# One order of a vision layer's attention steps: both images' scores together, both images' weighted sums together

## The chip, the cores and the metric

One core of a Trainium2 chip runs the program. The metric is the device time in microseconds, as the median of several executions. In the text an *image* is one of 16 inputs of 256 tokens, and a *pair* is two images that are worked on together (pairs 0 to 7).

## The reference

The layer cuts images of 5x128x128 into 256 patches and embeds them to 256 features with a layer norm. Then follows attention with a decay in place of a softmax, for 16 heads of 64, and then a mixture of 8 experts of which each token uses two. Cut to the attention, which the change is about:

```python
q, k = silu(x @ Wq), silu(x @ Wk);  v = x @ Wv          # 16 heads of 64
cum = cumsum(-softplus(x @ Wa + ba), axis=1)
decay = exp(where(causal, cum[i] - cum[j], -inf))
attn = (q @ k.T) * decay
o = attn @ v
o = group_norm(o) * gn_w + gn_b
out = (o * sigmoid(x @ Wg)) @ Wo
```

After it come a residual, a layer norm, a router (softmax, the two best of eight), and for each expert gelu(x w1 + b1) w2 + b2, weighted and added to the residual.

## The kernel before

The order of work is written out by hand, engine by engine, with semaphores between the engines. All eight pairs go through eight steps each (`step(p, c)`, c from 0 to 7; the last one is `last_step(p)`). A step works on two heads, c for both images of pair p. Work of other stages rides along in the steps: the embedding of the next pair (`tokens`, `embed`, `embed_norm`, `turn`, `scaled_h`), the norm, gate and output projection of the pair before (`gn_mean`, `gated`, `y_hi`, `y_lo`, `out_proj`, `residual`, `turn2`), and the routing of that pair and the one before it (`route`, `keep_logits`, `choose`, `place`, `scatter`).

In a step TensorE computes the scores of image u (`scores`, L1246 to L1258) into banks 4 and 5, one for each head; the projections for the two heads of step c+1 (`queries` into bank 0, `keys` into bank 1, `gates` into bank 2, L1212 and L1219; `values` into bank 0, 1 or 2), each of six matmuls, since an operand is split into a high and a low part; and the weighted sums (`weighted`, L1260 to L1274) into bank 3. Scores use 64 rows of the array for each head and weighted sums 64 columns for each head, so that the two heads' matmuls run beside each other; everything else uses the full 128x128. An f32 matmul of the trace's "x4" rows is two passes.

The order of TensorE in a plain step is: scores of image 0, queries, weighted sum of image 0, scores of image 1, keys, gates, weighted sum of image 1.

ScalarE computes tanh of q, k and g (`tanh_q` L828, `tanh_k` L833, `tanh_g` L840), exp of the decay rows (`decay`, L858, four to an image and step), and copies of v (L849) and o (`keep_o`, L863). `tanh_q` and `tanh_k` share one buffer, so that `tanh_k` waits for `silu_q`. VectorE computes `silu_q` and `silu_k` (L1731, L1738) and the product of scores and decays (`decayed`, L1747), two to an image. The product goes into a buffer for each head, `att`, which is why it waits for the weighted sum before it. GpSimd masks the decay rows (`decay_rows`, L684), two to an image, does the powers of the norms (L690, L695, L699) and scatters the normed rows to the experts' lists (`scatter`, L706). Each engine works through its list in order: an instruction that waits holds all behind it. The decay rows come from memory into a ring of `RING` = 4 slots, issued by SyncE two steps ahead, when the products have left a slot (`load_decay`).

After the attention come the experts' blocks: full blocks of 256 rows (`whole_row`, `mixed_row`: `layer1`, `layer2`, split operands) and unit blocks of 128 rows (`one_row`: `one1`, `one2`, plain f32), in turn at the end. Their sums leave PSUM with the bias added on VectorE (`keep_y`, L2004), are weighted on GpSimd (L735) and added to the output by an indirect DMA (L741, `add_rows`), each after the one before has landed. The last round is one full block and one unit block.

## Time and profile before

| | us |
|---|---|
| median of 3 runs | 1272.64 (1271.24 to 1274.25) |
| the profiled execution | 1270.91 |
| its span, first to last instruction | 1268.7 |
| TensorE busy | 1244.9 (98%) |
| ScalarE busy | 857.0 (68%) |
| VectorE busy | 827.5 (65%) |
| GpSimd busy | 429.8 (34%) |

The span has three parts: a start of 36.5 us, the attention steps to about 792, and the experts' blocks to the end. Matmuls are pipelined in the trace: a row of the timeline runs on under the next, so that the difference of two starts is what a group takes. The granted clock of TensorE is given as a share of its full 2.4 GHz.

### The profile page before, as it was taken

What the parts mean: (1) busy time and instruction counts of PE and PEld (TensorE: products, weight loads), DVE (VectorE), ACT (ScalarE), POOL (GpSimd) and SP (SyncE); (2) the same over time, 40 slices, a digit from 0 to 9 for tenths busy, and PEclk for the clock granted to TensorE, in tenths of its full rate; (3) what the DMA queues carried; (4) which work ended last, traced back from release to release, by engine and by line L of the source; (5) the groups of instructions that cost most, each with busy time, mean ns of one, the idle gap of its engine ahead of it and who ended that gap; (6) DMA issues with size and microseconds to landing.
All of it is one profiled execution on the core that took longest, in us unless ns stands there. A gap on an engine that the chain in (4) does not pass through costs nothing. (4 is left out here: it accounts for less than half of the span.)

```text
span 1268.7 us, 27357 instructions
## 1 busy us (share of the span) xinstructions
PE 1244.9 (98%) x8554; PEld 1070.0 (84%) x8554; DVE 827.5 (65%) x2123; ACT 857.0 (68%) x2019; POOL 429.8 (34%) x524
## 2 busy tenths in 40 slices
PE   8999999999999999999999999999999999999996
PEld 6677788787877877878877877989999999999995
DVE  5555565666667666666666566657888888566562
ACT  4766666667658567567577566547888888666672
POOL 2211121242142141242241241354454454443434
PEclk9999999999999999999999999999999999999998
DMA  5532222233233242232231337388988886999983
GB/s 191 169 106 81 95 90 89 83 114 111 81 116 111 67 130 87 85 124 78 93 126 49 124 109 231 111 230 241 300 223 246 226 223 188 260 273 277 262 244 86
DMA packets 125607, 194.46 MB, mean 153 GB/s; under 512 B 16272, under 2 KB 91504, under 8 KB 125360
## 3 DMA queue, kind: packets, MB, share of 16 engines
q1 hardware_dynamic: 110864, 175.37, 43.5%
q0 software_dynamic: 13584, 17.26, 6.8%
q8 instruction: 54, 0.88, 0.3%
q10 hardware_dynamic: 1056, 0.55, 0.2%
q14 instruction: 49, 0.40, 0.1%
HBM read 167.40 MB, written 29.05 MB: 155 GB/s over the span
## 5 line engine op out<-in xcount | busy, mean ns | idle before, releaser
L1219 PE MATMUL bank<-xn_sp,big_r 128*128 128x512 f32 x1152 | 312.5, 408 | 1.0 <-DVE xn_sp L1719 1.0
L1219 PEld LDWEIGHTS bank<-xn_sp,big_r 128*128 128x128 f32 x1152 | 204.9, 189 | 54.2 <-issue 1.7
L1747 DVE TENSOR_TENSOR att<-bank,dec_x 128x384 f32<-128x384 f32 x256 | 130.4, 550 | 99.2 <-PE bank L1258 94.3
L858 ACT ACTIVATE dec_x<-dec_x,ncum 128x256 f32<-128x256 f32 (+1 forms) x512 | 189.8, 445 | 5.8 <-POOL dec_x L684 5.8
L684 POOL TENSOR_SCALAR_AFFINE_SELECT dec_x<-dec_x 128x256 f32<-128x256 f32 x256 | 110.0, 458 | 215.1 <-DMA dec_x<-cum_scratch 214.7
L1565 PE MATMUL bank<-big_r 128*128 128x256 f32 x1296 | 167.5, 285 | 1.6 <-DVE big_r L2016 1.6
L1565 PEld LDWEIGHTS bank<-big_r 128*128 128x128 f32 x1296 | 160.4, 192 | 2.9 <-DVE big_r L2016 2.0
L741 POOL DMA_INDIRECT out<-mid_f,tok x71 | 120.4, 1696 | 59.8 <-issue 20.3
L735 POOL TENSOR_SCALAR mid_f<-mid_f,dec_x 128x256 f32<-128x256 f32 x71 | 75.8, 1073 | 169.8 <-DVE mid_f L2004 167.4
L928 ACT ACTIVATE mid_f<-bank,h 128x256 f32<-128x256 f32 x216 | 101.3, 479 | 33.6 <-PE bank L1565 20.0
L828 ACT ACTIVATE tq<-bank 128x512 f32<-128x512 f32 x64 | 38.3, 598 | 113.0 <-PE bank L1219 112.9
L2020 DVE TENSOR_TENSOR big_r<-mid_f,big_r 128x256 fp32r<-128x256 f32 x216 | 91.1, 424 | 33.8 <-ACT big_r L948 33.7
L2011 DVE TENSOR_TENSOR big_r<-big_f,big_r 128x512 fp32r<-128x512 f32 x148 | 102.0, 693 | 9.7 <-ACT big_r L922 2.2
L1297 PEld LDWEIGHTS bank<-big_r,y_sp 128*128 128x128 f32 x768 | 95.5, 191 | 1.9
L1212 PE MATMUL bank<-big_r,xn_sp 128*128 128x512 f32 x384 | 97.0, 392 | 0.0
L1297 PE MATMUL bank<-big_r,y_sp 128*128 128x256 f32 x768 | 96.8, 284 | 0.0
L833 ACT ACTIVATE tq<-bank 128x512 f32<-128x512 f32 x64 | 38.2, 597 | 86.1 <-PE bank L1219 86.0
L922 ACT ACTIVATE big_r<-big_f 128x512 fp32r<-128x512 f32 x148 | 93.7, 637 | 2.8 <-DMA big_f<-in_L_ffn_w 2.6
L948 ACT ACTIVATE big_r<-mid_f 128x256 fp32r<-128x256 f32 x216 | 91.9, 426 | 0.0
L1255 PE MATMUL bank<-q_s,k_s 64*128 64x256 f32 x512 | 90.0, 428 | 0.3 <-DVE k_s L1738 0.3
L706 POOL DMA_INDIRECT expert_rows<-xn,slot x64 | 65.5, 1023 | 72.9 <-DVE slot L1882 56.7
L1269 PE MATMUL bank<-att,mid_f 128*64 128x256 f32 x512 | 84.8, 404 | 3.9 <-DVE att L1747 2.8
(237 smaller groups left out, 2225.4 us busy)
## 6 DMA issues: line engine op xcount, KB each, us to landing
big_f<-in_L_ffn_w SPq DMA_DIRECT2D x68, 1024.0 KB, 7.3
dec_x<-cum_scratch SPq DMA_DIRECT2D x128, 384.0 KB, 3.6
big_w<-in_L_ffn_w SPq DMA_DIRECT2D x12, 1024.0 KB, 7.7
mid_f<-expert_rows SPq DMA_DIRECT2D x27, 261.0 KB, 3.1
h_scratch<-h SPq DMA_DIRECT2D x16, 256.0 KB, 2.2
h<-h_scratch SPq DMA_DIRECT2D x8, 512.0 KB, 4.4
out<-h SPq DMA_DIRECT2D x16, 256.0 KB, 4.0
xt<-in_x SPq DMA_DIRECT2D x14, 256.0 KB, 3.8
```

The source lines that it names most:

```text
L684: pool.affine_select(out=d, in_=d, pattern=[[0, 2], [1, P]], compare_op=ALU.is_ge, fill=fill, base=0, channel_multiplier=-1).then_inc(M["c ...
L741: pool.indirect_dma_start(out=out_rows, out_offset=bass.IndirectOffsetOnAxis(ap=tok[k.par][:, s:s + 1], axis=0), in_=yo[k.par][:, s, :], i ...
L858: act.activation(d, d, ACT.Exp, bias=ncum[p % 2][:, NS * u + s, 2 * c + hh:2 * c + hh + 1]).then_inc(M["exp_done"], 1)
L922: act.activation(parts[0].rearrange("p k n -> p (k n)")[:, cols], staged[:, cols], ACT.Copy).then_inc(M[f"{name}_hi"], 1)
L928: act.activation(target, bank[hbank[c % HB]][:, 0:width], ACT.Gelu_apprx_tanh, bias=b1_sb[k.par][:, c:c + 1]).then_inc(M["gel_done"], 1)
L948: act.activation(g_sp[0][:, c, :], gel[c % NGEL], ACT.Copy).then_inc(M["gh_done"], 1)
L1212: mm = pe.matmul(bank[target][:, :], xp[:, k, t * P:(t + 1) * P], wp[:, k, n * 512:(n + 1) * 512], start=(k == 0 and j == 0), stop=(k == E ...
L1219: mm = pe.matmul(bank[target][:, :], wp[:, k, c * P:(c + 1) * P], xp[:, k, :], start=(k == 0 and j == 0), stop=(k == EC - 1 and j == 2))
L1297: mm = pe.matmul(bank[target][:, s * E:(s + 1) * E], yp[:, j, u * S + s * P:u * S + (s + 1) * P], wp[:, GC * g + j, :], start=(j == 0 and ...
L1565: mm = pe.matmul(bank[hbank[c % HB]][:, 0:BLK], wp[:, i, c * P:(c + 1) * P], xp[:, i, :], start=(i == 0 and j == 0), stop=(i == EC - 1 and ...
L1747: dve.tensor_tensor(att[hh][:, :], bank[4 + hh][:, 0:LW], dec[n % RING][:, hh, :], ALU.mult).then_inc(M["mult_done"], 1)
L2011: dve.tensor_tensor(lo, staged[:, cols], f32(hi), ALU.subtract).then_inc(M[f"{name}_lo"], 1)
```

## The change

- TensorE's plain step becomes: scores of image 0, scores of image 1, gates, queries, keys, weighted sum of image 0, weighted sum of image 1. The scores of image 1 go to the banks of queries and keys (0 and 1; in the very first step 6 and 3).
- `queries` and `keys` of the next step therefore wait for the third and the fourth product of this one; `values` always go to bank 2.
- VectorE's product overwrites the decay row in its slot, the buffers `att` are gone, and the ring has five slots, which come free after the weighted sum.
- ScalarE's order: the decay of the next step's image 0 and tanh of g stand ahead of tanh of q (in step 5 and in the very first step it stays behind); `keep_x2` of the second image and `xn_hi` move; `decay` of image 1 stays behind tanh of k.
- VectorE does the four products first in a step, with `affine_steps`, `spread`, `running_sums` and the rest behind; `keep_logits` of the first image comes behind `silu_q` in step 6.
- The last step of a pair, and the first expert block's early part (`turn_first` into bank 6), follow the same pattern.
- In the last round both halves of the full block's second layer come before the unit's first layer, and VectorE multiplies with the weights while it reads PSUM (`weighted_bias`, `keep_weighted`), so that GpSimd only scatters.

The removed lines of `step` and `last_step` are left out: they are the lines of the kernel before that do not return.

```diff
@@ -46,7 +46,7 @@
-RING = 4
+RING = 5
...
@@ -328,6 +327,12 @@
             if n > 0:
                 eng.wait_ge(M[name], n)
+        def score_bank(p, c, u, hh):
+            if u == 0:
+                return bank[4 + hh]
+            return bank[(6, 3)[hh]] if p == 0 and c == 0 else bank[hh]
         def pair(n):
             return 0 <= n < NPR
...
@@ -387,7 +392,7 @@
             def load_decay(p, c, u):
                 n = 2 * NP * p + 2 * c + u
-                have(sp, "mult_done", 2 * (n - RING + 1))
+                have(sp, "o_ps", n - RING + 1)
                 sp.wait_ge(M[f"cum_out{u}"], 48 * (p + 1))
                 rows = cum_d[p, u:u + 1, 2 * c:2 * c + 2, :].rearrange("a h n -> a (h n)")
                 sp.dma_start(dec[n % RING].rearrange("p h n -> p (h n)"), rows.broadcast_to([P, 2 * LW])).then_inc(M[f"dec_in{n % RING}"], 16)
...
@@ -948,62 +963,67 @@
                 act.activation(g_sp[0][:, c, :], gel[c % NGEL], ACT.Copy).then_inc(M["gh_done"], 1)
             def last_step(p):
+                nxt = pair(p + 1)
+                keep_o(p, 6)
+                if pair(p - 1):
+                    keep_x2(2 * p - 1)
+                y_hi(p, 0, 0)
                 if nxt:
+                    tanh_g(p + 1, 0)
                     y_hi(p, 0, 1)
                     tanh_q(p + 1, 0)
                     keep_v(p + 1, 0, 2)
+                    tanh_k(p + 1, 0)
+                    keep_v(p + 1, 1, 2)
                     decay(p + 1, 0, 0)
+                    decay(p + 1, 0, 1)
+                else:
+                    x_early(0)
                     keep_o(p, 7)
+                    y_hi(p, 0, 1)
                     active_early(0, 0)
             def step(p, c):
+                nxt, post, routed = pair(p + 1), pair(p - 1), pair(p - 2)
                 if c == 7:
                     last_step(p)
                     return
+                if c > 0:
                     keep_o(p, c - 1)
+                elif post:
+                    keep_o(p - 1, 7)
                 if c == 4 and nxt:
                     keep_xnT(2 * p + 3)
                 if c == 6 and post:
                     keep_x2(2 * p - 2)
                 if c == 5 and nxt:
                     softplus(p + 1)
+                late = c == 5 or (p, c) == (0, 0)
+                if not late:
                     decay(p, c + 1, 0)
+                tanh_g(p, c + 1)
                 if c in (1, 2) and post:
                     affined(p - 1, 1, c - 1)
                 if c == 3 and post:
                     y_hi(p - 1, 1, 1)
+                if c == 6:
                     affined(p, 0, 0)
+                tanh_q(p, c + 1)
+                if c == 0 and p > 0:
+                    keep_v(p, 2, 2)
+                if c in (1, 2, 3):
+                    keep_v(p, {1: 4, 2: 6, 3: 7}[c], 2)
+                tanh_k(p, c + 1)
+                if c == 0 and p > 0:
+                    keep_v(p, 3, 2)
+                if c == 1:
+                    keep_v(p, 5, 2)
+                if c == 6 and nxt:
+                    keep_cum(p + 1)
+                    xn_hi(p + 1)
+                if late:
+                    decay(p, c + 1, 0)
+                decay(p, c + 1, 1)
                 if c == 0 and routed:
                     top_exp(2 * p - 4)
                     top_exp(2 * p - 3)
...
@@ -1011,12 +1031,8 @@
                     y_hi(p - 1, 1, 0)
                 if c == 3 and nxt:
                     scaled_h(2 * p + 3)
-                if c == 6 and nxt:
-                    keep_cum(p + 1)
-                if c == 6 and main:
+                if c == 6:
                     affined(p, 0, 1)
-                if main:
-                    tanh_g(p, c + 1)
                 if c == 1 and nxt:
                     keep_xnT(2 * p + 2)
                     scaled_h(2 * p + 2)
...
@@ -1225,52 +1241,60 @@
                     pe.wait_ge(M["ws_lo"], 1)
                 pe.wait_ge(M["xl_done"], p + 1)
                 have(pe, "sq_done", NP * p + c)
-                have(pe, "v_done", 2 * TP * p + {1: 2, 3: 6, 4: 7}.get(c, 0))
+                if (p, c) != (0, 1):
+                    have(pe, "mult_done", 4 * (NP * p + c - 1) + 3)
                 project(0, 0, c, "q_ps")
             def keys(p, c):
                 if p == 0 and c == 0:
                     pe.wait_ge(M["ws_lo"], 3)
                 have(pe, "sk_done", NP * p + c)
-                have(pe, "v_done", 2 * TP * p + {1: 4}.get(c, 0))
+                if (p, c) != (0, 1):
+                    have(pe, "mult_done", 4 * (NP * p + c - 1) + 4)
                 project(1, 1, c, "k_ps")
             def gates(p, c):
                 if p == 0 and c == 0:
                     pe.wait_ge(M["ws_lo"], 4)
+                pe.wait_ge(M["xl_done"], p + 1)
                 have(pe, "tg_done", NP * p + c)
-                have(pe, "v_done", 2 * TP * p + {0: 1, 1: 3, 2: 5, 4: 8}.get(c, 0))
+                have(pe, "v_done", 2 * TP * p + {0: 0 if p > 0 else 1, 1: 2, 2: 4, 3: 6, 4: 7, 5: 8}.get(c, 0))
+                have(pe, "h2a_done", 2 * p if c == 1 else 0)
                 project(2, 3, c, "g_ps")
...
+                    pe.matmul(score_bank(p, c, u, hh)[:, 0:S], k[r, 0:P], q[r, :], start=True, stop=True)
+                    pe.matmul(score_bank(p, c, u, hh)[:, S:LW], k[r, P:S], q[r, P:S], start=True, stop=True).then_inc(M["s_ps"], 1)
...
@@ -1384,97 +1414,83 @@
             def last_step(p):
                 main, nxt = pair(p), pair(p + 1)
+                scores(p, 7, 0)
+                scores(p, 7, 1)
                 if pair(p + 2):
                     tokens(2 * p + 4)
+                if pair(p - 1):
                     route(2 * p - 1)
+                if p == NPR - 1:
+                    turn_first()
                 if nxt:
+                    gates(p + 1, 0)
                     queries(p + 1, 0)
+                    values(p + 1, 0, 2, "tg_done", NP * (p + 1) + 1)
                     keys(p + 1, 0)
+                    values(p + 1, 1, 2, "v_done", 2 * TP * (p + 1) + 1)
                     out_proj(p, 0, 0, 7, "lg_done", 2 * p)
+                    out_proj(p, 0, 1, 2, "v_done", 2 * TP * (p + 1) + 2)
+                weighted(p, 7, 0)
+                weighted(p, 7, 1)
+                if p == NPR - 1:
+                    early1(0, 0)
             def step(p, c):
+                nxt, post, routed = pair(p + 1), pair(p - 1), pair(p - 2)
                 if c == 7:
                     last_step(p)
                     return
+                scores(p, c, 0)
+                scores(p, c, 1)
+                gates(p, c + 1)
                 if c == 1 and routed:
                     ranks(p - 2, *(("gv_done", 2 * p) if post else ("taken_done", p - 2)))
                 if c == 2 and nxt:
                     tokens(2 * p + 3)
                 if c == 4 and post:
                     out_proj(p - 1, 1, 0, 7, *(("taken_done", p - 1) if routed else ("gv_done", 2 * p)))
+                if c == 5:
                     gn_mean(p, 0, "h2_done", 2 * p)
                 if c == 6 and nxt:
                     cum(p + 1)
                 if c == 6 and post:
                     route(2 * p - 2)
+                queries(p, c + 1)
+                if c == 0 and post:
+                    gn_mean(p - 1, 1, "h2a_done", 2 * p - 1)
+                if c == 0 and p > 0:
+                    values(p, 2, 2, "tg_done", NP * p + 2)
+                if c == 1:
+                    values(p, 4, 2, "tg_done", NP * p + 3)
+                if c == 2:
+                    values(p, 6, 2, "tg_done", NP * p + 4)
+                if c == 3:
+                    values(p, 7, 2, "tg_done", NP * p + 5)
+                if c == 4 and nxt:
+                    logits(p + 1)
+                if c == 6 and nxt:
+                    cum_rows(p + 1)
+                keys(p, c + 1)
                 if c == 0 and post:
                     gn_var(p - 1, 1)
+                if c == 0 and p > 0:
+                    values(p, 3, 2, "v_done", 2 * TP * p + 3)
+                if c == 1:
+                    values(p, 5, 2, "v_done", 2 * TP * p + 5)
                 if c == 1 and nxt:
                     turn(2 * p + 2)
                 if c == 3 and nxt:
                     turn(2 * p + 3)
                 if c == 4 and post:
                     out_proj(p - 1, 1, 1, 7, "h2_done", 2 * p - 1)
+                if c == 5:
+                    gn_var(p, 0)
                 if c == 5 and post:
                     turn2(2 * p - 2, "s1_z", min(p + 2, NPR), 6)
+                if c == 6 and post:
+                    turn2(2 * p - 1, "lg_done", 2 * p - 1)
+                weighted(p, c, 0)
+                weighted(p, c, 1)
             tokens(0)
             tokens(1)
...
@@ -1650,7 +1669,11 @@
             with pe.Fori(1, ROUNDS) as r:
                 two_rounds(r)
             m0, u0 = four(ROUNDS)[0:2]
-            mixed_row(m0, 0, u0)
+            layer1(m0, 0, two)
+            turn_rows(u0, rows_f[1], 1)
+            layer2(m0, 0, one)
+            layer2(m0, 0, two)
+            one1(u0, one)
             one1(u0, two)
             one2(u0, one)
             one2(u0, two)
...
@@ -1741,10 +1764,10 @@
             def decayed(p, c, u):
                 n = 2 * (NP * p + c) + u
                 dve.wait_ge(M["exp_done"], 4 * (n + 1))
-                have(dve, "o_ps", n)
                 for hh in range(2):
                     dve.wait_ge(M["s_ps"], 2 * n + hh + 1)
-                    dve.tensor_tensor(att[hh][:, :], bank[4 + hh][:, 0:LW], dec[n % RING][:, hh, :], ALU.mult).then_inc(M["mult_done"], 1)
+                    d = dec[n % RING][:, hh, :]
+                    dve.tensor_tensor(d, score_bank(p, c, u, hh)[:, 0:LW], d, ALU.mult).then_inc(M["mult_done"], 1)
             def head_stats(p, c):
                 dve.wait_ge(M["o_done"], NP * p + c + 1)
...
@@ -2004,6 +2027,22 @@
...
+            def keep_weighted(k, pieces, count):
+                dve.wait_ge(M["y_ps"], k.j + 1)
+                dve.wait_ge(M["yb_done"], count)
+                for s in range(pieces):
+                    dve.scalar_tensor_tensor(out=yo[k.par][:, s, :], in0=bank[6][:, s * E:(s + 1) * E], scalar=wsel[k.par][:, s:s + 1],
+                                             in1=yo[k.par][:, s, :], op0=ALU.mult, op1=ALU.add).then_inc(M["ys_done"], 1)
```

Left out of the diff are the same edits elsewhere (names, semaphores, VectorE's reordered `step`, whose order is told above). VectorE's list behind `silu_k` in a step (`gated` in steps 1 and 2, `embed` in steps 0 and 2) and GpSimd's list keep their order.

## Rows read from the trace of the kernel before

**Rows 1.** The page's busy times, shares of the span and instructions.
```profile
PE 1244.9 (98%) x8554; PEld 1070.0 (84%) x8554; DVE 827.5 (65%) x2123; ACT 857.0 (68%) x2019; POOL 429.8 (34%) x524
```

**Rows 2.** Windows: length, busy of PE, PEld, DVE, ACT, POOL, PEclk, DMA.
```profile
36.50:792.30 755.80, 751.37 (x4869) 595.89 (x4869) 477.33 (x1197) 501.82 (x1135) 207.30 (x347) 1.00 0.33 106
418.92:517.12 98.20, 98.20 (x640) 78.70 (x639) 63.28 (x166) 64.80 (x147) 28.59 (x46) 1.00 0.31 99
```

**Rows 3.** Timeline of PE: start, length, instructions, in two middle steps.
```profile
403.40 0.65 PE L1269 MATMUL bank<-att,mid_f 128*64 128x256 f32 x4
...
404.20 0.70 PE L1255 MATMUL bank<-q_s,k_s 64*128 64x256 f32 x4
...
405.05 1.66 PE L1219 MATMUL bank<-xn_sp,big_r 128*128 128x512 f32 x6
406.55 1.54 PE L1212 MATMUL bank<-big_r,xn_sp 128*128 128x512 f32 x6
...
450.08 1.55 PE L1212 MATMUL bank<-big_r,xn_sp 128*128 128x512 f32 x6
451.46 1.52 PE L1219 MATMUL bank<-xn_sp,big_r 128*128 128x512 f32 x6
452.91 0.65 PE L1269 MATMUL bank<-att,mid_f 128*64 128x256 f32 x4
```

**Rows 4.** Timeline of DVE, from silu of k to the first product of step 3.
```profile
450.91 0.69 DVE L1738 SCALAR_TENSOR_TENSOR k_s<-tq,bank 128x512 f32<-128x512 f32 x1 [1.12 <-ACT tq L833]
451.51 1.22 DVE L1789 SCALAR_TENSOR_TENSOR big_f<-big_f 128x1024 f32<-128x1024 f32 x1
...
455.28 1.02 DVE L1747 TENSOR_TENSOR att<-bank,dec_x 128x384 f32<-128x384 f32 x2
```

**Rows 5.** Timeline of ACT, the decay of step 4.
```profile
457.24 1.50 ACT L858 ACTIVATE dec_x<-dec_x,ncum 128x256 f32<-128x256 f32 x4 [0.36 <-POOL dec_x L684]
```

**Rows 6.** Timeline of DVE: silu of q, slots, and products of pair 7.
```profile
445.06 0.69 DVE L1731 SCALAR_TENSOR_TENSOR q_s<-tq,bank 128x512 f32<-128x512 f32 x1 [0.49 <-ACT tq L828]
...
447.33 0.17 DVE L1882 SCALAR_TENSOR_TENSOR slot<-idxf,rsel 128x8 uint32<-128x8 f32 x1
...
747.88 1.01 DVE L1747 TENSOR_TENSOR att<-bank,dec_x 128x384 f32<-128x384 f32 x2
```

**Rows 7.** Timeline of PE, a matmul that waited for a product.
```profile
748.57 0.80 PE L1269 MATMUL bank<-att,mid_f 128*64 128x256 f32 x3 [0.22 <-DVE att L1747]
```

**Rows 8.** Timeline of POOL around step 3.
```profile
448.32 1.03 POOL L706 DMA_INDIRECT expert_rows<-xn,slot  x1 [6.39 <-DVE slot L1882]
...
452.19 1.38 POOL L706 DMA_INDIRECT expert_rows<-xn,slot  x1 [0.30 <-issue]
455.42 1.04 POOL L690 TENSOR_TENSOR rs<-rs,mhalf 128x4 f32<-128x4 f32 x1 [1.85 <-DVE rs L1681]
456.44 1.48 POOL L684 TENSOR_SCALAR_AFFINE_SELECT dec_x<-dec_x 128x256 f32<-128x256 f32 x4
```

**Rows 9.** Timeline of ACT in step 6.
```profile
487.63 0.60 ACT L863 ACTIVATE big_f<-bank 128x512 f32<-128x512 f32 x1 [0.40 <-PE bank L1273]
...
491.93 1.08 ACT L871 ACTIVATE big_f<-big_f,gbi,gsc 128x256 f32<-128x256 f32 x2
```

**Rows 10.** Timeline of PE, its last two runs.
```profile
1251.11 1.95 PE L1590 MATMUL bank<-xs,big_f 128*128 128x128 f32 x16
1252.89 3.62 PE L1601 MATMUL bank<-big_f,q_s 128*128 128x256 f32 x16
```

**Rows 11.** Timeline of DVE, its last instruction.
```profile
1256.55 0.42 DVE L2004 TENSOR_TENSOR mid_f<-bank,tq 128x256 f32<-128x256 f32 x1 [3.77 <-PE bank L1601]
```

**Rows 12.** Timeline of POOL, the last three scatters.
```profile
1254.97 1.61 POOL L741 DMA_INDIRECT out<-mid_f,tok  x1 [0.85 <-issue]
1256.88 1.56 POOL L741 DMA_INDIRECT out<-mid_f,tok  x1 [0.30 <-issue]
...
1261.59 1.60 POOL L741 DMA_INDIRECT out<-mid_f,tok  x1 [2.17 <-DMA out<-mid_f,tok]
```

More of the change, by code:

```diff
@@ L770, in _ @@
                 two_rounds(r)
[L771 to L772 removed]
+            add_weighted(four(ROUNDS)[0], BS, 0)
+            add_weighted(four(ROUNDS)[1], 1, BS)
         @block.scalar
@@ L1150, in keep_running @@
                 for i in range(n):
-                    pe.matmul(bank[5][:, 0:E], att[0][:, 0:P], att[0][:, P:P + E], start=True, stop=True)
+                    pe.matmul(bank[5][:, 0:E], dec[0][:, 0, 0:P], dec[0][:, 0, P:P + E], start=True, stop=True)
             pe.wait_ge(M["cleared"], 1)
```

256 lines of the change are left out of this document (88 added, 168 removed).

## The prediction

> **What bounds the kernel now.** I read the page's busy line first: TensorE holds 98% of the span and no other engine over 68% [rows 1]. Then the busy time by stretch: the reader should see that in a middle pair of images (418.92 to 517.12) TensorE is busy for the whole 98.20 us at full clock, and over all the attention steps for 751.4 of 755.8 us, so only some 4.4 us of waiting are to be had there [rows 2]. The chain of waits shows the end as a chain of GpSimd instructions and output transfers after the last matmul (the 2.17 us of idle before the last scatter) [rows 12]. So two things can move the time: what TensorE itself loses between its instructions, and the end. The PE timeline shows the loss. In it the starts count: a row's own time runs on under the next.
>
> **What the joined runs save.** A step now has, twice, scores (matmuls of 64 rows), full-size projections, weighted sums (128x64), scores again. Without a change of shape, passes of 256 columns follow each other every 0.216 us ((3.62-0.38)/15) and passes of 128 columns every 0.11 [rows 10]. The two heads of a group run side by side, so a group should take 2x0.216 + 2x0.11 = 0.65. The score group takes 405.05-404.20 = 0.85, the weighted group 404.20-403.40 = 0.80. A projection between two others takes 451.46-450.08 = 1.38, one ahead of a weighted group 452.91-451.46 = 1.45, one behind a score group 406.55-405.05 = 1.50 [rows 3]: 0.12 on the way in, 0.07 on the way out. One score and one weighted group less to enter and leave: 0.20+0.15+0.12+0.07 = 0.54 us a step. In the seven last steps with another pair behind them the old order also returns to full shape between the groups and before the next pair's scores, 0.2 more each. 64x0.54 + 7x0.2 = 36.0 us. Bounds: 12 if the joined groups drain at the seam as well (the 0.20 and 0.15 stay), 40 at most. I take 36.0, as the 128-column passes inside a group already follow each other without it.
> The Trainium skill (TensorEngine Tiling, Key Properties) says that a change of tiling mode drains the engine, and "TensorE: Matmul & The Clock Gate", Single matmul latency, gives a lone matmul 398 cycles beside its columns, 166 ns. Three changes less in 64 steps at that price would be 32 us (an estimate from that page), against 36.0 by the rows; the rows decide.
> The products in place have the same form and size as before (0.55 us each, one every 0.47) and I cost that edit at nothing (nearest rows: the two take 1.01) [rows 6]. The fifth slot frees the decay row a step early; its transfer has a step of 9 us or more to land, so nothing too.
>
> **What the new order makes wait.** The second image's scores go to the banks of q and k. So the queries of the next step wait for the third product and the keys for the fourth, with only one projection (gates) between; scores wait for silu of k with only the joined weighted group before them; values wait for tanh of g, which ScalarE now does behind the next step's decay. I followed each step with the durations of rows.
> Step 3 is the place. Call K the end of silu of k for step 3 (451.60). It ended 1.52 after the group behind the keys began (450.08, 450.91 + 0.69) [rows 3, 4]; the joined weighted group takes 2x0.65 and the 0.22 around it, 1.5, so scores start at about K+0.1. TensorE is done with both scores and gates at K+0.1+1.5+0.1+1.4 = K+3.1. But VectorE, which is off the path today, has behind silu_k: gated, then embed of the next pair; its first product of step 3 starts at 455.28 = K+3.68 [rows 4]. The third ends at K+3.68+2x0.47+0.55 = K+5.17 and TensorE restarts 0.15 later (a matmul at 748.57 after a product begun at 747.88 for 0.55 [rows 6, 7]): **2.2 us of waiting**. Next, values 7 needs the bank of g. ScalarE stands at decay of step 4, which needs GpSimd's mask: embed ends at K+3.7, power 1.04, two masks, decay starts at 457.24 = K+5.64 [rows 5, 8], tanh of g ends 1.4+0.6 later, K+7.7, and queries end at K+6.7: **1.0 more**. From pair 2 on, the scatter of pair p-2 is ahead of that power on GpSimd. It starts 0.82 after the slots (447.50) and lasts 453.57-448.32 = 5.25 [rows 6, 8]. The slots follow silu of q by 1.75 (445.75), today 4.1 before K. In the new order only values 6 and keys lie between queries and the next group, so silu of q ends 2x1.38 = 2.8 before K and the slots are ready 1.05 before it. So the scatter ends at K+5.0, the power at 6.1, masks 6.8, decay 8.3, tanh 8.9: **2.3 in place of 1.0**. What is late next is turn, by 0.2. Step 3 loses 4.7 in pairs 2 to 6, 3.5 in pair 1, 2.0 in pair 0 (no gated), and in pair 7 (tables in place of embed, first product 747.88 = K+4.9) 3.45+0.9, with 0.9 ahead of it since the tokens no longer cover the slots.
> Step 6: the logits of the last route leave bank 7 behind silu of q, and that waits for tanh of q, now behind keep_o, keep_x2, decay, tanh of g and four affines. ScalarE comes out of step 5 at 1.36 after the scores start (decay twice 1.39 from tanh of k); 1.36+0.49+0.49+1.39+0.49+1.97+0.60 = 6.8 (keep_o 487.63, affine 1.08 for two [rows 9], the rest alike), silu 7.5, copy and turn2 at 7.75, where keys end at 7.05: 0.7 a pair, 1.25 in pair 0 (there scores wait for k), 1.05 in pair 7. Last step: route waits for keep_x2, now behind the affines; tokens (12 passes of 0.216, 2.6 us) cover it in pairs 1 to 5, in pair 6 it costs 2.5, in pair 7 1.35.
> Small ones: pair 0, steps 0 to 2: scores behind k 0.6, queries behind embed 1.1, values 4 behind tanh of g 1.1, weight 4 0.85; pair 1 step 1, 0.7; scores of step 3 0.1 a pair. Steps 0, 1, 4 and 5 of the others come out covered by 0.2 to 0.4 us only.
> Sum of new waits: pair 0 6.9; pair 1 5.0; pairs 2 to 5 5.5 each, 22; pair 6 8.0; pair 7 7.65; together 49.6. Each is bounded below by nothing, where the covers hold, and above by about twice, where thin covers fail too. Old waits that go: 4.4. Attention: -36.0-4.4+49.6 = **+9.2**.
>
> **The end.** The last full block's second layer now follows its first half without the unit's first layer between (a run of sixteen such passes takes 1252.89-1251.11 = 1.8 [rows 10]), so its sums are complete at 1249.3 in place of 1251.1. VectorE weighs them out of PSUM (two pieces, 0.42 each, by the unit's last copy [rows 11]), and GpSimd's two products go. First scatter at about 1250.7 (within the 0.85 that preceded it today) in place of 1254.97, the second 1.9 later at 1252.6. Today the last scatter starts 4.7 after the second [rows 12], when that has landed; now it may at 1257.3. The unit's last matmul still ends at 1256.4; weighed at 1257.0, scattered at 1257.6: **-4.0** (bounds -3 and -4.5).
>
> **Sum.** The profiled execution took 1270.91 (span 1268.7): 1270.9+9.2-4.0 = 1276.1. The median of the runs shown, 1272.64, is 1.7 above the profiled one, so the forecast is 1278.
>
> **The rivals.**
> A: only the bank waits bite and ScalarE's does not, because masks and decays come earlier than I put them (for: GpSimd is busy only 34%; against: in step 3 the mask stands behind embed already today [rows 5, 8]). It decides once the mask of step 4 is there by K+3.5. Minus 2.3x5+1.0x2+0.9 and half of step 6, 3: 1278-17 = 1261.
> B: the waits are nearly all covered, VectorE reaching its products in time: 36.0+4.4+4.0 gained, some 15 of the 49.6 left: 1272.6-29 = 1243. For: VectorE is busy 65%; against: the 3.68 us between silu of k and the first product in step 3 is a queue, not an average.
> C, the other side by another way: the two waits of step 3 stand 1.4 us apart and the granted clock falls to 1.2 GHz there. It stayed 1.00 through all of 36.5 to 792.3, waits included [rows 2], so I give it little. A projection at half clock costs 1.4 more; two or three of them in seven pairs are 20 to 29: about 1300. The Trainium skill ("TensorE: Matmul & The Clock Gate", HAM oscillation) states that waits repeated in a loop of matmuls let the clock fall again; no row before the end shows it.
> D: the thin covers of steps 0, 1, 4 and 5 fail too, 0.3 us in each: 32x0.3 = 10, 1288.
>
> **How the numbers follow.** Forecast 0.50 (own range 1270 to 1286), A 0.19, B 0.14, C 0.06, D 0.11. 0.2% is 2.5 us, about what a measurement of this kernel can tell from no change. Faster: B, most of A, and little of the forecast's range, 0.31; same: 0.17, the low part of the forecast's range and a part of A; slower: the rest of it, C and D, 0.52. Range 1252 to 1289, which leaves out most of B and C.
>
> **What would show it.** Right: between pairs 2 and 5, TensorE idle twice in step 3, first for about 2.2 us before queries, released by a product, then about 2.3 before values 7, released by tanh of g; in step 6 0.7 before turn2; a pair of about 99 us (98.2 before); 8 score matmuls in 1.5 us; the last scatter starting 4 us nearer to the last matmul. Wrong: joined groups of 1.7 us (no gain), a pair under 96 us (A or B), or a granted clock under 1.00 between 36 and 790.

## The result, and the profile of the changed kernel

The changed kernel takes 1283.9 us (median of 6 runs, 1281.99 to 1289.28), the kernel before, on the same chip, 1273.22 (6 runs, 1271.24 to 1274.95): a ratio of 1.0082, 95% interval 1.0065 to 1.0099. It is slower by 10.7 us. Forecast were 1278 (1252 to 1289), a loss of 5.4 against the 1272.64 known then; the sign came as forecast, the size about twice as large.

The page of the changed kernel, its busy line and its clock line (40 equal slices):

```profile
PE 1223.3 (95%) x8554; PEld 1067.8 (83%) x8554; DVE 823.2 (64%) x2127; ACT 859.5 (67%) x2019; POOL 417.8 (33%) x521
...
PEclk9999999989999999999999989999999999999999
```

Against [rows 1]: TensorE is busy for 21.6 us less, and stands idle in 5% of the span where it stood idle in 2%. The windows of the attention steps and of pair 4, columns as in [rows 2]:

```profile
35.24:802.60 767.36, 725.29 (x4821) 589.87 (x4821) 467.15 (x1187) 500.43 (x1129) 199.91 (x347) 0.99 0.32 103
421.73:520.52 98.79, 94.83 (x641) 77.91 (x639) 62.70 (x166) 65.06 (x147) 27.72 (x46) 1.00 0.30 99
```

A middle pair takes 98.79 us against 98.20 [rows 2], now with 4 us of idle time in it; pairs 3 to 5 agree within 0.03. Counting from the start of the first scores of pair 0 to the start of the scores of pair 7's last step, the attention grew from 749.98 us (36.50 to 786.48) to 767.36: **+17.4**. It starts 1.3 earlier, the stretch from there to TensorE's end takes 0.6 more, and what follows the last matmul is 3.8 shorter: together +12.9, and the profiled execution took 1283.67 in place of 1270.91.

Step 3 of pair 4 on the PE timeline (start, length), the answer to [rows 3]:

```profile
453.71 0.65 PE L1293 MATMUL bank<-dec_x,mid_f 128*64 128x256 f32 x4
...
455.24 0.70 PE L1277 MATMUL bank<-q_s,k_s 64*128 64x256 f32 x4
...
456.74 1.66 PE L1235 MATMUL bank<-xn_sp,big_r 128*128 128x512 f32 x6
460.43 1.61 PE L1235 MATMUL bank<-xn_sp,big_r 128*128 128x512 f32 x6 [2.03 <-issue]
463.77 1.63 PE L1228 MATMUL bank<-big_r,xn_sp 128*128 128x512 f32 x6 [1.73 <-ACT big_f L854]
465.24 1.53 PE L1235 MATMUL bank<-xn_sp,big_r 128*128 128x512 f32 x6
```

Both joined groups take 1.5 us (453.71 to 455.24 to 456.74). Then come the two waits: 2.03 before queries and 1.73 before values 7 (tanh of g is L854). Their releasers, first on the DVE timeline (product in place, L1770), then on ACT (decay L872, tanh of g), then on POOL (scatter L711, power L695, mask L689), the answers to [rows 4, 5, 8]:

```profile
458.80 1.95 DVE L1770 TENSOR_TENSOR dec_x<-bank,dec_x 128x384 f32<-128x384 f32 x4
```

```profile
461.66 1.49 ACT L872 ACTIVATE dec_x<-dec_x,ncum 128x256 f32<-128x256 f32 x4 [4.44 <-POOL dec_x L689]
463.06 0.57 ACT L854 ACTIVATE big_f<-bank 128x512 f32<-128x512 f32 x1
```

```profile
458.85 0.96 POOL L711 DMA_INDIRECT expert_rows<-xn,slot  x1 [0.30 <-issue]
459.83 1.05 POOL L695 TENSOR_TENSOR rs<-rs,mhalf 128x4 f32<-128x4 f32 x1
460.86 1.48 POOL L689 TENSOR_SCALAR_AFFINE_SELECT dec_x<-dec_x 128x256 f32<-128x256 f32 x4
```

The waits of PE by releaser, costliest first (us in total, times, longest), over the whole kernel; L1235 is queries, keys and gates, L1228 values, L1332 turn2, L1340 the route:

```profile
PE bank L1228 <- ACT big_f L854: 11.7, 10, 1.7
PE bank L1235 <- issue: 10.2, 5, 2.1
PE bank L1235 <- DVE dec_x L1770: 8.3, 5, 3.0
PE bank L1332 <- DVE lg L1849: 6.3, 7, 5.2
PE bank L1277 <- issue: 2.7, 4, 1.2
PE bank L1340 <- ACT turned L897: 2.4, 1, 2.4
```

The 10.2 us put down to "issue" at L1235 are the same wait as the 8.3 below them: in the run named late, where it is unchanged, the profile puts all 18.4 down to the product. One entry was not in the forecast at that size, 5.2 us at turn2, in step 6 of pair 7. Its chain stands on SP's queue (L413 and L417 are expert weights, L398 a decay row), POOL and PE; the first row of SP and the first of POOL are the decay row ahead of the weights and its mask:

```profile
778.14 0.32 SPq L398 DMA_DIRECT2D dec_x<-cum_scratch  x1
780.06 0.41 SPq L413 DMA_DIRECT2D big_w<-in_L_ffn_w  x1
780.57 0.42 SPq L417 DMA_DIRECT2D big_w<-in_L_ffn_w  x1
...
784.95 0.39 SPq L398 DMA_DIRECT2D dec_x<-cum_scratch  x1
```

```profile
781.81 0.77 POOL L689 TENSOR_SCALAR_AFFINE_SELECT dec_x<-dec_x 128x256 f32<-128x256 f32 x2 [5.21 <-DMA dec_x<-cum_scratch]
...
792.72 0.78 POOL L689 TENSOR_SCALAR_AFFINE_SELECT dec_x<-dec_x 128x256 f32<-128x256 f32 x2 [4.70 <-DMA dec_x<-cum_scratch]
```

```profile
798.80 1.12 PE L1332 MATMUL bank<-ident,xn 128*128 128x128 f32 x4 [5.15 <-DVE lg L1849]
```

The decay row at 784.95 is issued 4.9 us behind the first weights and lands 7.8 us after its issue, where the mask of the row ahead of the weights could start 3.7 after that row's issue (778.14 to 781.81). ScalarE's decay starts on it at 793.52, tanh of q stands behind that at 797.36; silu of q, the copy of the logits and turn2 follow. In the kernel before the weights stood ahead of the same row too, but both were issued earlier in the steps:

```profile
764.50 0.41 SPq L408 DMA_DIRECT2D big_w<-in_L_ffn_w  x1
...
770.04 0.33 SPq L393 DMA_DIRECT2D dec_x<-cum_scratch  x1
```

The scores of step 6 began 6.5 us behind that row's issue there (776.58), and 1.9 behind it in the changed kernel (786.81). Last, three windows in which the granted clock was half, 1.2 GHz (half-clock stretches from here on):

```profile
261.70:268.50 6.80, 5.55 (x14) 3.89 (x13) 1.52 (x4) 4.00 (x8) 5.69 (x10) 0.50 0.23 80
756.70:763.50 6.80, 6.02 (x15) 4.10 (x16) 0.69 (x1) 3.19 (x7) 4.39 (x6) 0.50 0.22 80
797.60:804.40 6.80, 5.60 (x30) 4.00 (x32) 2.64 (x5) 5.96 (x13) 0.00 (x0) 0.50 0.92 315
```

They are in step 3 of pair 2, in step 3 of pair 7 and at pair 7's turn2; between 36.5 and 792.3 the kernel before had a granted clock of 1.00 [rows 2]. Pair 2 took 100.88 in place of 98.79, so the stretch cost about 2.1 there.

The end, the answer to [rows 10 to 12], on PE, DVE and POOL:

```profile
1269.64 3.62 PE L1620 MATMUL bank<-big_f,q_s 128*128 128x256 f32 x16
```

```profile
1273.30 0.48 DVE L2043 SCALAR_TENSOR_TENSOR mid_f<-bank,dec_x,mid_f 128x256 f32<-128x256 f32 x1 [5.06 <-PE bank L1620]
```

```profile
1274.62 1.57 POOL L755 DMA_INDIRECT out<-mid_f,tok  x1 [3.56 <-DVE mid_f L2043]
```

The last scatter starts 1.36 behind the last matmul's end (1269.64+3.62), where it started 5.08 behind it: 3.7 less.

### The profile page after: what moved, and what is told of

It is laid out like the page before. It is cut to its first block, busy times and chain, and to the rows that moved or that the text cites. A ratio compares the mean times of both kernels' runs of the same rounds, so it can differ in the third digit from the quotient of the medians.

```text
span 1281.7 us, 27365 instructions
## 1 busy us (share of the span) xinstructions
PE 1223.3 (95%) x8554; PEld 1067.8 (83%) x8554; DVE 823.2 (64%) x2127; ACT 859.5 (67%) x2019; POOL 417.8 (33%) x521
## 4 chain that ended last, share of the span: by engine, by line
PE 77%; ACT 7%; issue 4%; DVE 4%; POOL 3%; DMA 2%; SPq 0%; ACTq 0%; POOLq 0%; another core or an unknown queue 0%; DVEq 0%
PE bank L1235 15%; PE bank L1581 11%; PE bank L1593 11%; PE bank L1321 7%; PE bank L1228 7%; PE bank L1293 4%; PE bank L1277 4%; ACT dec_x L872 3%; PE bank L1185 3%; PE bank L1620 2%; PE bank L1606 2%; PE bank L1395 2%; PE bank L1408 2%; POOL expert_rows L711 2%; PE bank L1297 2%
## 5 line engine op out<-in xcount | busy, mean ns | idle before, releaser
L1235 PE MATMUL bank<-xn_sp,big_r 128*128 128x512 f32 x1152 | 305.5, 406 | 19.0 <-issue 10.2
L1235 PEld LDWEIGHTS bank<-xn_sp,big_r 128*128 128x128 f32 x1152 | 210.1, 190 | 70.5 <-issue 23.1
L689 POOL TENSOR_SCALAR_AFFINE_SELECT dec_x<-dec_x 128x256 f32<-128x256 f32 x256 | 104.0, 432 | 385.4 <-DMA dec_x<-cum_scratch 385.3
L872 ACT ACTIVATE dec_x<-dec_x,ncum 128x256 f32<-128x256 f32 (+1 forms) x512 | 188.2, 444 | 45.7 <-POOL dec_x L689 45.7
L1581 PE MATMUL bank<-big_r 128*128 128x256 f32 x1296 | 167.5, 285 | 1.6 <-DVE big_r L2055 1.6
L1770 DVE TENSOR_TENSOR dec_x<-bank,dec_x 128x384 f32<-128x384 f32 x256 | 124.9, 550 | 39.3 <-PE bank L1280 34.0
L1754 DVE SCALAR_TENSOR_TENSOR q_s<-tq,bank 128x512 f32<-128x512 f32 x64 | 44.0, 688 | 137.6 <-ACT tq L842 116.1
L746 POOL DMA_INDIRECT out<-mid_f,tok x68 | 113.7, 1672 | 52.7 <-issue 17.6
L1228 PE MATMUL bank<-big_r,xn_sp 128*128 128x512 f32 x384 | 102.6, 404 | 11.7 <-ACT big_f L854 11.7
L1228 PEld LDWEIGHTS bank<-big_r,xn_sp 128*128 128x128 f32 x384 | 71.6, 192 | 30.4 <-issue 16.4
L711 POOL DMA_INDIRECT expert_rows<-xn,slot x64 | 63.5, 993 | 77.1 <-DVE slot L1905 60.9
L1277 PE MATMUL bank<-q_s,k_s 64*128 64x256 f32 x512 | 84.5, 405 | 2.7 <-issue 2.7
L1593 PE MATMUL bank<-big_r 128*128 128x256 f32 x672 | 86.7, 285 | 0.2 <-issue 0.2
```

What stands on the lines that cost most here:

```text
L689: pool.affine_select(out=d, in_=d, pattern=[[0, 2], [1, P]], compare_op=ALU.is_ge, fill=fill, base=0, channel_multiplier=-1).then_inc(M["c ...
L746: pool.indirect_dma_start(out=out_rows, out_offset=bass.IndirectOffsetOnAxis(ap=tok[k.par][:, s:s + 1], axis=0), in_=yo[k.par][:, s, :], i ...
L872: act.activation(d, d, ACT.Exp, bias=ncum[p % 2][:, NS * u + s, 2 * c + hh:2 * c + hh + 1]).then_inc(M["exp_done"], 1)
L1228: mm = pe.matmul(bank[target][:, :], xp[:, k, t * P:(t + 1) * P], wp[:, k, n * 512:(n + 1) * 512], start=(k == 0 and j == 0), stop=(k == E ...
L1235: mm = pe.matmul(bank[target][:, :], wp[:, k, c * P:(c + 1) * P], xp[:, k, :], start=(k == 0 and j == 0), stop=(k == EC - 1 and j == 2))
L1277: pe.matmul(score_bank(p, c, u, hh)[:, 0:S], k[r, 0:P], q[r, :], start=True, stop=True)
```

## The experiments

Diffs are against the changed kernel unless said otherwise. The kernel before ran beside each of the three groups: 1272.15 (with the first four), 1273.66 (with the next four and again with the last two). The groups thus differ by up to 1.5 us in the kernel before, and a difference between runs of different groups is no surer than that. The stretch ahead of the first scores, which none of the edits on the changed kernel touches, took 35.24 us (changed kernel) to 39.51 (unjoin) in the profiled executions, so these are compared from the first scores on.

**late: tanh of g ahead of the decay in step 3.**

```diff
-                late = c == 5 or (p, c) == (0, 0)
+                late = c in (3, 5) or (p, c) == (0, 0)
```

> The changed kernel with one edit: in step 3 ScalarE does the decay of the next step's image 0 behind tanh of k, as in step 5. Theory 1 (the second wait of step 3 is tanh of g held by a decay that waits for GpSimd's mask): the wait before values 7 (1.7 us from pair 2 on, about 1 in pairs 0 and 1) goes, step 3 of pairs 2 to 6 falls from 13.4 to about 11.5 us, the whole by some 12 us, to about 1271, and a half-clock stretch may go with it. Rival (values 7 waits for the bank or for queries in any case): step 3 stays at 13.4, 1284.

Measured: 1277.19, ratio 1.0039 (1.0026 to 1.0052). The waits of PE:

```profile
PE bank L1235 <- DVE dec_x L1770: 18.4, 10, 3.0
...
PE bank L1228 <- ACT big_f L854: 1.2, 2, 0.8
```

The wait on tanh of g is gone (11.7 to 1.2), which shows that it is ScalarE's queue behind GpSimd's mask; the wait on products stays (18.4, against 10.2 and 8.3 before the edit). The time is 6 above the 1271 of the theory. Step 3 took 11.35 in pairs 1 and 5 and 12.95 in pairs 3, 4 and 6, though the waits in all of them are alike. The difference is the clock, as in pair 6:

```profile
651.70:655.10 3.40, 3.40 (x10) 2.62 (x9) 1.41 (x4) 0.60 (x1) 2.91 (x5) 0.50 0.14 47
```

Such stretches of 3.4 us lie in step 3 of pairs 3, 4, 6 and 7 and at pair 6's route, and one of 6.8 at pair 7's turn2, where the changed kernel had three of 6.8. In pairs 3, 4 and 6 the stretch took back 1.6 of the 2.1 that step 3 had won, and at pair 6's route it cost 1.6 as well (20.69 against 19.09). The median is 6.7 lower; in the profiled execution the attention is 10.5 shorter and the start 2.1 longer.

**embed: the next pair's embedding behind the products of step 3.**

```diff
                 decayed(p, c, 1)
+                if c == 3 and nxt:
+                    embed(2 * p + 3)
+                if c == 3 and p == NPR - 1:
+                    first_tables()
...
-                    if nxt:
-                        embed(2 * p + 3)
-                    if p == NPR - 1:
-                        first_tables()
```

> The changed kernel with one edit: VectorE does embed (and in pair 7 the first tables) behind the four products of step 3 and not ahead of them. Theory 1 (the two waits of step 3 are in line: the power and mask for the next decay follow embed): the wait before queries (2.1 us) goes, but power, mask, decay and tanh of g come later, so the wait before values 7 takes its place and more, step 3 about 14.6 us, the whole some 5 us slower than the changed kernel, about 1289. Rival (the waits are independent): 2.1 us a pair less, about 1269.

Measured: 1308.59, ratio 1.0290 (1.0257 to 1.0323). The wait on products went (L1235 on L1770: 2.4 left) and the other grew to three and a half times its size:

```profile
PE bank L1228 <- ACT big_f L854: 40.7, 10, 5.2
```

The power, and with it mask, decay and tanh of g, needs what embed computes. So the theory had the chain and the sign, but with 1289 only a fifth of the loss. Step 3 took 15.6 to 17.1, and the clock was half in it in all eight pairs, as here in pair 3, where the wait ended at 377.16:

```profile
375.30:382.10 6.80, 4.94 (x12) 3.91 (x13) 1.41 (x3) 3.74 (x8) 5.12 (x8) 0.50 0.22 79
```

This is what rival C of the prediction describes, in all pairs, but behind one wait of 4.2 to 5.2 us in place of two short ones. The Trainium skill ("TensorE: Matmul & The Clock Gate", HAM oscillation) tells of a loop of matmuls in which a wait for data lets the clock fall at every pass. This trace agrees (0.50 in step 3 of all eight pairs); the changed kernel, which waits in every step 3 too, for 1.7 to 3.8 us in all, had it in two of eight.

**both: late and embed together.**

> The changed kernel with the tanh of g of the step behind step 3 ahead of the decay on ScalarE (as in late) and the embedding of the next pair behind the four products of step 3 on VectorE (as in embed). Theory (the two waits of step 3 are queues of two engines, and each edit alone leaves the other one): first product at K+1.9 in place of K+3.7, queries start without a wait; tanh of g no longer stands behind the mask, which comes later by the 1.9 that embed moves; turn is late by at most 0.8. Step 3 at 9.9 to 10.6 in place of 13.42, no stretch at half clock in steps 3, attention minus 20 to 24, 1260 to 1264. Rival (the waits only move: embed late makes mask, decay, affines and turn late by the 5 us that embed showed when alone): step 3 at 12 or more, 1275 to 1285, half-clock stretches stay.

Measured: 1255.31, ratio 0.9847 (0.9826 to 0.9869): 28.6 less than the changed kernel, where the one edit alone gave 6.7 and the other lost 24.7 (29.9, 5.5 and 26.5 if each is taken against the kernel before beside it). That is 5 better than the theory's best. Step 3 of pair 4 on the PE timeline, and the window up to pair 6:

```profile
445.43 3.04 PE L1235 MATMUL bank<-xn_sp,big_r 128*128 128x512 f32 x12
448.31 1.52 PE L1228 MATMUL bank<-big_r,xn_sp 128*128 128x512 f32 x6
449.67 1.52 PE L1235 MATMUL bank<-xn_sp,big_r 128*128 128x512 f32 x6
451.85 0.63 PE L1194 MATMUL bank<-ident,turned 128*128 128x128 f32 x4 [0.66 <-DVE turned L1713]
```

```profile
36.29:682.60 646.31, 632.58 (x4262) 519.06 (x4263) 416.21 (x1036) 444.60 (x998) 183.42 (x304) 1.00 0.33 103
```

Gates and queries run as twelve matmuls without a gap, values 7 follows, and of the waits of step 3 only 0.66 at turn is left. Step 3 takes 9.9 in place of 13.4, a middle pair 95.3 in place of 98.8, and the clock holds until 682.6. So the two waits are two queues of one chain, and each edit alone leaves or lengthens the other.

**block: the first expert weights issued behind the decay rows of the last step.**

```diff
-                    if p == NPR - 1 and c == 4:
+                    if p == NPR - 1 and c == 5:
                         first_block()
```

> The changed kernel with one edit: in pair 7 SyncE issues the first expert's weights and rows behind the decay rows of step 5 and not of step 4. Theory 1 (in pair 7 the decay rows of step 7 are issued behind 2 MB of weights, since their slot now comes free a step's end later): step 6 of pair 7 falls from 15.8 to about 10.3 us and the half-clock stretch at 798 goes, the whole 6 to 9 us faster than the changed kernel, about 1276. Rival (step 6 waits for ScalarE's backlog): no change, 1284.

Measured: 1282.37, ratio 1.0080 (1.0059 to 1.0101). The 5.2 at turn2 is gone (the group's longest wait is 0.7). On SP's queue the decay row that stood ahead of the weights and the one that stood behind them now go out together:

```profile
780.22 0.97 SPq L398 DMA_DIRECT2D dec_x<-cum_scratch  x2
```

Step 6 of pair 7 fell from 15.79 to 9.61, which shows the order on SP's queue as the cause. But the time did not move clear of noise (1.5 lower, ratios 1.0080 and 1.0082), so that the rival's 1284 is nearer than the theory's 1276 although its reason is refuted. In the profiled execution the attention is 5.9 shorter and the start 1.8 longer, and in the attention half-clock stretches lay in steps 3 of pairs 2, 3 and 4 (13.59, 13.40, 15.08) and of pair 7, and at pair 6's route; pairs 2 to 6 came out 1.4 longer together, the route of pair 7 now waits itself (1.3), and from the start of the last step's scores to TensorE's end it is 472.3 in place of 470.7. In pairs 2 and 3 the wait before values 7 took up part of the slow matmuls: it was 0.52 and 0.46 there and 1.72 in pair 5, which kept the full clock.

**tail: the kernel before, with the last round's change alone** (both halves of the second layer first, weights applied while PSUM is read, GpSimd only scatters).

> The kernel before with the last round's part of the change alone (both halves of the full block's second layer first, weights applied by VectorE). Theory: -3.7 to -4 us against before, 1269.4, with the last scatter 4 us nearer to the last matmul. Rival (the end is set by GpSimd and the landing in any order): within 1 us of before.

Measured: 1270.13, ratio 0.9979 (0.9966 to 0.9992). Behind the last matmul it is 3.8 shorter, as in the changed kernel; the span is 2.6 shorter; this run also had a half-clock stretch of 3.4 us at 696.8, right behind a wait of 1.1 that the kernel before has too, at full clock. The last round's part is a gain by itself, of 2.0 in the median where the theory had 3.7 to 4.

**unjoin: the first image's weighted sum ahead of the keys again.**

```diff
+                weighted(p, c, 0)
                 keys(p, c + 1)
...
-                weighted(p, c, 0)
                 weighted(p, c, 1)
```

> The changed kernel with the first image's weighted sum put ahead of the keys again, so that only the second image's stands ahead of the scores. Priced by the rows of before: a weighted group entered and left between two projections costs 0.15 for its own drain, 0.12 on the way in and 0.07 on the way out, 0.34 us a step, 22 us in 64 steps. Theory (the joining is worth what the prediction puts it at): 1284 + 22, less what the group fills of waits that now stand behind it (keys wait for the fourth product in the first steps, silu of k has 0.75 less beside it and costs up to 0.3 a step): 1300 to 1312. Rival (a change of shape costs nothing by itself, and the 0.54 was the order): 1284 give or take 4.

Measured: 1325.10, ratio 1.0389 (1.0362 to 1.0416): 41 more than the changed kernel, beyond both expectations. What the shape costs can be read in step 5 of pair 3, first the changed kernel's step 5 of pair 4, then this one's:

```profile
486.67 3.00 PE L1235 MATMUL bank<-xn_sp,big_r 128*128 128x512 f32 x12
...
490.21 0.65 PE L1293 MATMUL bank<-dec_x,mid_f 128*64 128x256 f32 x4
...
491.66 0.70 PE L1277 MATMUL bank<-q_s,k_s 64*128 64x256 f32 x4
```

```profile
410.06 1.63 PE L1235 MATMUL bank<-xn_sp,big_r 128*128 128x512 f32 x6
411.62 0.65 PE L1293 MATMUL bank<-dec_x,mid_f 128*64 128x256 f32 x4
...
412.42 1.68 PE L1235 MATMUL bank<-xn_sp,big_r 128*128 128x512 f32 x6
...
414.64 0.65 PE L1293 MATMUL bank<-dec_x,mid_f 128*64 128x256 f32 x4
...
415.55 0.70 PE L1277 MATMUL bank<-q_s,k_s 64*128 64x256 f32 x4
```

Projections, gt and turn2 up to the last group: 3.54 joined, 1.56+2.22 = 3.78 unjoined. The groups: 1.45 joined, 0.80+0.80 and 0.11 of waiting for silu of k unjoined. So a second entry costs 0.24+0.15 = 0.39, where 0.34 was put. In step 4 the group stands behind other small matmuls, and the step grew by 0.23 in all. The edit adds such an entry in steps 0 to 6, not in the last step: 56 in all, not the 64 that the expectation counts. At 0.23 to 0.39 they are 13 to 22 of the 34.4 us by which the attention grew (767.36 to 801.73). The rest went to waits that the same order lengthened (scores after silu of k 2.7 to 11.6, the first weighted sum itself 0 to 6.2, route 2.4 to 6.4) and to half-clock stretches; the start and what follows the attention took 8 more in this execution. The price of a shape change is shown, the run's whole loss only in outline.

**logits: the copy of the logits ahead of silu of q in step 6.**

```diff
+                if c == 6 and post:
+                    keep_logits(2 * p - 2)
                 silu_q(p, c + 1)
...
-                if c == 6 and post:
-                    keep_logits(2 * p - 2)
                 silu_k(p, c + 1)
```

> The changed kernel with the copy of the last route's logits ahead of silu of q in step 6 on VectorE. Theory (in step 6 turn2 waits for the copy only because the copy stands behind silu of q, which waits for tanh of q): the 0.2 a pair of waiting at turn2 in pairs 1 to 6 and part of pair 7's 5.2 go, since there silu of q waits for affines and decay rows; 1.2 + some 4 to 5: 1279. Rival (queries' tanh is late anyway, so scores wait in place of turn2): 1284, within 1 us; the wait in pair 7 shows at the scores or the turn.

Measured: 1288.16, ratio 1.0108 (1.0084 to 1.0132). The turn2 wait went and came back at the scores (issue, 5.7 with one of 3.0) and at the route (4.8 in place of 2.4): as the rival says. The median is 4.3 higher, more than the rival gave, but the intervals of the two ratios overlap, so that a loss is not shown. A middle pair is 0.17 shorter; from the start of the last step's scores to TensorE's end 475.5 passed in place of 470.7, with the route's second wait of 2.0 and a half-clock stretch at 806.7 in it. What else lengthened it stays open.

**best: both, block and logits together.**

> The changed kernel with four orders changed: tanh of g ahead of decay in step 3, embed behind the products of step 3, the last block's first weights issued behind the decay rows of the last step, and the logits copied ahead of silu of q. Theory (each is a queue with something not urgent in front): 1262 for the first two, minus 5 to 6 for pair 7's step 6, minus 1: about 1255, no stretch at half clock between 36 and 780, which beats the kernel before by 17. Rival (the waits move on, and the clock falls elsewhere as it did in the runs named late and block): 1265 to 1275.

Measured: 1256.01, ratio 0.9853 (0.9824 to 0.9883), no better than both. In the profiled execution the attention is 7.9 shorter than in both (730.3 against 738.2), but the start is 3.1 longer, the route now waits in pair 7 too, a half-clock stretch of 6.8 us begins right behind that wait (773.3), and from the start of the last step's scores to TensorE's end it is 477.4 in place of 469.8. The time is the theory's (1255) by luck: it put both at 1262, which came at 1255.3, and 6 to 7 more for the other two edits, which brought nothing in the time. What the rival describes, waits and a slow clock that move on, is what the trace shows, but its 1265 to 1275 did not come.

**route and best2: the second image's affines behind keep_x2** (route: on top of late, embed and block; best2: with logits as well).

```diff
                     keep_x2(2 * p - 1)
+                affined(p, 0, 1)
                 y_hi(p, 0, 0)
...
-                if c == 6:
-                    affined(p, 0, 1)
```

> The run named both, with the last block's first weights issued behind the decay rows of the last step (as in block), and in step 6 the four affines of the second image's part moved behind the copies of the last step (keep_o and keep_x2) on ScalarE. The run named both took 1255.3, with 2.4 of waiting at the route in pair 6 (released by keep_x2) and 2.9 at turn2 in pair 7. Theory (the route waits because keep_x2 stands behind affines, and the weights in front of the decay rows cost pair 7 its turn2 wait): pair 6 loses its route wait (-2.4), step 6 of pair 7 falls from 13.3 to about 9.6 and the route of pair 7 no longer waits either (-3.7): 1255.3 - 6 = 1249. Rival (what pair 7 gains is given back in the expert blocks, whose first weights now land later): pair 7 shorter by 3.7, the stretch from the last scores to TensorE's end longer by as much (468.7 in both): 1253.

> The run named best (1256.0: both, block and logits together) with the same four affines moved behind keep_o and keep_x2. In best the route waited 2.8 in pair 6 and 2.0 in pair 7, and half-clock stretches stood right behind the wait in pair 7 (773 to 780). Theory: both waits go (-4.8), the half-clock stretch behind the second goes with them (-3): 1256 - 7 = 1249, and within 2 us of the run named route, since logits alone moved nothing. Rival (the copy of logits ahead of silu of q makes scores late by 0.2 to 0.4 in the last step of each pair): route is faster by 1 to 3, best2 1250 to 1252.

Measured: route 1250.26, ratio 0.9815 (0.9787 to 0.9844); best2 1247.42, ratio 0.9792 (0.9767 to 0.9817); both within 2 of their theories. The waits of PE in best2, the two costliest and, from 600 to 800 us, the route's; L1193 is the turn, L1276 scores, L1339 the route:

```profile
PE bank L1193 <- DVE turned L1712: 5.7, 8, 2.0
PE bank L1276 <- issue: 4.4, 6, 1.6
```

```profile
PE bank L1339 <- ACT turned L897: 0.8, 1, 0.8
```

Of the route's waits 0.8 is left in pair 6 (0.4 in the run route) and none in pair 7, where best had 2.8 and 2.0; from the start of the last step's scores to TensorE's end route takes 470.1, so the rival of a later end is out. In best2, between 19.1 and 1237, the clock was at full speed throughout. best2 is 2.8 below route, their ranges overlap (1248.15 to 1253.42, 1245.44 to 1249.7), so what logits adds here is not settled. best2 beats the kernel before by 26 us and the changed kernel by 36.

## Why the prediction was right, and where it was not

- **Joined groups: right in steps 4 and 5, a little large over a pair.** Both took 1.5 as worked out from [rows 3, 10], steps 4 and 5 of a middle pair got 0.56 and 0.51 shorter for the 0.54 put down, and unjoin gave 0.39 for the 0.34 of one entry. Steps 0, 1 and 2 got 0.33, 0.46 and 0.50. In best2, with hardly a wait, TensorE is busy for 33.0 us less than in the kernel before (1211.9), for the 36.0 forecast.
- **Step 3, first wait: right.** 2.2 forecast, 2.03 in pair 4. With K the end of silu of k (455.1: on DVE the next instruction starts at 455.05), the products start at K+3.7 as put.
- **Step 3, second wait: right in place and chain, 0.6 too long.** 1.73 for 2.3. Power at K+4.7 for K+5.0 forecast, mask at K+5.8, decay at K+6.6, tanh of g over at K+8.5 for K+8.9.
- **A middle pair: right, in part by luck.** 98.79 for "about 99". Two terms were off and met: 5.5 of waits were put and 3.9 came (2.03, 1.73 and 0.19), and 4.5 of saving was put where 3.4 is left once those waits are taken off (98.21 to 98.79-3.95). Rival A (ScalarE's wait absent) and B (all covered) are out by these rows.
- **Step 6 and the last step: partly.** 0.7 a pair was put before turn2 and 0.2 came. The route in pair 6 waited 2.4 for 2.5 forecast. In pair 7 the route's 1.35 did not show in the changed kernel, because turn2 had already waited; with that gone it was 1.3 in block and 2.0 in best.
- **The end: right.** 3.8 shorter behind the last matmul, and the last scatter 3.7 nearer to it, for 4.0.
- **The step that failed: "The fifth slot frees the decay row a step early; its transfer has a step of 9 us or more to land, so nothing too."** The transfer was looked at alone and not the queue in front of it. The second image's row for step 6 is now issued behind a weighted sum, at the end of step 4: at 778.14, 0.5 ahead of the scores of step 5, where it went 5.4 ahead of them in the kernel before (762.57, scores at 767.94). The expert weights stand behind it on SP's queue in both kernels, and the first row for step 7 behind them. So in the changed kernel this row goes out 6.3 us into step 5 in place of 2.1, though its slot is free by the start of the step (block issues it at once), and it lands 7.8 us after its issue. Step 6 of pair 7 took 15.79 and, in the order of block, 9.61: 6.2 us for this order, the half-clock stretch at 797.6 included.
- **The clock, given 0.06 as rival C, came in part.** Three half-clock stretches of 6.8 us; the first cost 2.1. C was priced for all pairs or none: with the same waits, pairs 3 to 6 kept the full clock and pair 2 did not. The windows of before [rows 2] could not tell, since the longest wait in its attention was 1.6. The prediction says that no row before the end shows a fall; the trace of the kernel before has one, of 3.4 us, in the start (23.9).

In sum, up to the start of the last scores, the attention came to +17.4. The forecast's +9.2 holds pair 7's last step too; without it, and without the old wait there, it is 9.0. Pair 7 was put at 7x0.54 and an old wait of 0.2 less and 6.3 more, +2.3, and it took 84.7 against 73.8: +10.9. So pair 7 was put 8.6 too low, by 5.4 in step 6, by 2.2 in step 3, with the half-clock stretch in it, and by 0.9 in step 4. Pair 2's clock is 2.1 more. All else in pairs 0 to 6 came out 2.3 shorter than put, which hides a part of both. Rival D's thin covers did not fail in a middle pair: no wait is left in its steps 0, 1, 4 and 5.

## What to carry to other kernels

A wait in front of TensorE can be two queues deep, as here: remove one and the other shows, so edit the chain together (6.7 gained and 24.7 lost singly, 28.6 gained jointly). When buffers come free at another time, follow each refill on the issuing queue together with everything that stands behind it and ahead of it, in the last pass as well as in the middle one. A wait of 2 us between matmuls cost up to 3.6 here, since the clock may fall with it (late).

## What the runs showed of the hardware

- The granted clock fell to half behind waits of some 2 us or more, and once, in tail, behind one of 1.1. Half-clock stretches between 36 us and the last scores: none in the kernel before (4.4 us of waits in all [rows 2]), three of 6.8 us in the changed kernel (two in its eight steps 3, with 3.4 and 3.8 us of waits, one at a wait of 5.2), five of 3.4 and one of 6.8 in late (four in its steps 3, with waits of 2.0 and once 3.0), nine in embed (eight in its steps 3, behind one wait of 4.2 to 5.2), none in best2. The same waits in the same order met a full and a half clock in different pairs; what decides between them was not settled.
- What a stretch costs depends on the waits that it meets. One of 3.4 us cost 1.6 in late, and nothing in pair 3 of block (13.40 with it, 13.41 in pair 5 without), where the wait before values 7 fell from 1.72 to 0.46. One of 6.8 cost 2.1 in pair 2 of the changed kernel and 1.7 in pair 4 of block.
- A decay row (384 KB by the page's DMA issues) that was issued 4.9 us behind the first of two weight loads of 1024 KB on one queue landed after 7.8 us, the one ahead of them after 3.7. With the weights behind both (block) it no longer held up TensorE.
- Where matmuls of full shape would otherwise follow each other, a lone weighted group costs 0.39 more than its matmuls' own passes take: 0.24 at its edges and 0.15 within.
